# A decoder kernel: the step sizes of its state-space stage from a 32-column projection

## The reference

```
zxbcdt = X @ W_in.T
z, xBC, dt = split(zxbcdt)            # 1024 z, 1152 xBC, 16 dt
dt = softplus(dt + dt_bias)           # step sizes, one for each of 16 heads
xBC = silu(conv1d(xBC) + conv_b)      # 4 taps
x, B, C = split(xBC)
h[t] = h[t-1] * exp(dt[t] * A) + dt[t] * B[t] * x[t]
y[t] = C[t] . h[t] + D * x[t]
y = rmsnorm(y * silu(z)) * norm_w
out = y @ W_out.T
```

## Time and profile before

| | |
|---|---|
| median of three runs | 2119.28 us |
| profiled execution | 2113.45 us |
| its span on the core | 2111.7 us |
| PE busy | 1977.2 us, 94% |
| DVE busy | 1455.6 us, 69% |
| ACT busy | 1222.7 us, 58% |
| POOL busy | 390.4 us, 18% |
| instructions | 40222 |

### The profile page before, as it was taken

How to read it: one execution, slowest core, us unless ns; L and a number is a source line. 1 busy time by engine, 2 the same in 40 slices (tenths; PEclk the granted TensorE clock), 3 DMA queues, 4 the chain that set the end, 5 groups by cost and what they waited for, 6 DMA issues and landing times. The chain is left out here.

```text
span 2111.7 us, 40222 instructions
## 1 busy us (share of the span) xinstructions
PE 1977.2 (94%) x13484; PEld 1339.6 (63%) x13484; DVE 1455.6 (69%) x2887; ACT 1222.7 (58%) x3068; POOL 390.4 (18%) x596
## 2 busy tenths in 40 slices
PE   7899999999999999858999999999999999889988
PEld 6667676767676767535566666666665655478853
DVE  7978787878786868525757676757576767556438
ACT  4435354444444453316878787878778786546614
POOL 1110111111111010230122222222212132200006
PEclk9999999999999999888999999999999999999999
DMA  6122222222221313232334333333333332631157
GB/s 211 53 59 79 60 79 60 79 52 87 50 88 41 98 27 91 81 113 63 101 81 121 81 112 86 104 91 105 98 91 101 88 97 71 190 135 61 60 189 269
DMA packets 120291, 200.72 MB, mean 95 GB/s; under 512 B 23072, under 2 KB 44576, under 8 KB 120096
## 3 DMA queue, kind: packets, MB, share of 16 engines
q1 hardware_dynamic: 110880, 179.20, 28.3%
q0 software_dynamic: 9216, 18.89, 3.6%
HBM read 117.27 MB, written 29.88 MB: 70 GB/s over the span
## 5 line engine op out<-in xcount | busy, mean ns | idle before, releaser
L1751 ACT ACTIVATE a_shared<-a_shared,a_mx 128x512 f32<-128x512 f32 x512 | 341.6, 670 | 57.2 <-DVE a_mx L1812 57.2
L1744 ACT ACTIVATE a_probs<-a_scores 128x512 f32<-128x512 f32 x512 | 292.4, 605 | 96.5 <-PE a_scores L1954 94.4
L1812 DVE TENSOR_REDUCE a_mx<-a_shared 128x1 f32<-128x512 f32 x512 | 318.6, 682 | 14.4 <-PE a_shared L1938 13.4
L934 PE MATMUL m_proj<-m_xt_hi,link 128*128 128x512 f32 x576 | 241.8, 420 | 18.9 <-DVE m_xt_lo L655 11.0
L1954 PE MATMUL a_scores<-a_qs,a_ks 98*128 98x512 f32 x512 | 218.9, 435 | 21.6 <-ACT a_probs L1744 17.9
L1938 PE MATMUL a_shared<-a_ks,a_qs 96*128 96x512 f32 x512 | 216.2, 434 | 17.6 <-ACT a_shared L1751 13.4
L935 PE MATMUL m_proj<-m_xt_lo,link 128*128 128x512 f32 x576 | 230.7, 401 | 0.0
L936 PE MATMUL m_proj<-m_xt_hi,link 128*128 128x512 f32 x576 | 230.2, 400 | 0.0
L1076 PE MATMUL m_outp<-m_wout,m_g 128*128 128x512 f32 x512 | 226.3, 600 | 2.7 <-issue 2.7
L1912 PE MATMUL a_shared<-link 128*128 128x512 f32 x768 | 189.5, 399 | 18.6 <-POOL a_ks L1684 15.7
L463 ACT ACTIVATE m_acc<-m_proj,m_cb,m_cw 128x512 f32<-128x512 f32 x72 | 58.2, 818 | 254.0 <-PE m_proj L936 253.8
(11 more groups left out here) (259 smaller groups left out, 3437.1 us busy)
## 6 DMA issues: line engine op xcount, KB each, us to landing
m_dec<-step_decay SPq DMA_DIRECT2D x64, 256.0 KB, 4.0
a_qs<-link SPq DMA_DIRECT2D x256, 64.0 KB, 2.1
m_ce<-run_decay SPq DMA_DIRECT2D x128, 112.0 KB, 3.6
a_ks<-a_k_hi POOLq DMA_DIRECT2D x192, 64.0 KB, 2.4
e_x<-x SPq DMA_DIRECT2D x11, 1024.0 KB, 5.5
m_xt_in<-x_t_in SPq DMA_DIRECT2D x8, 1024.0 KB, 7.8
m_x_tok<-x_in SPq DMA_DIRECT2D x8, 1024.0 KB, 5.5
x<-m_x_tok SPq DMA_DIRECT2D x32, 256.0 KB, 2.2
```

The costliest lines, as they stand in the source:

```text
L934: pe.matmul(bank[:, :], wh, xt_hi[:, k, :], start=(k == 0), stop=False)
L1744: act.activation(probs[:, n % 2, h, :], scores[t.score_bank(n, h)][:, :], ACT.Exp, scale=-1.0).then_inc(exp_ready, 1)
L1751: act.activation(scored[:, :], scored[:, :], ACT.Exp, scale=-1.0, bias=mx[:, i % 2, j, h:h + 1], accum_out=den[:, i, j, h:h + 1]).then_inc ...
L1812: dve.tensor_reduce(mx[:, i % 2, j, h:h + 1], bank(what)[:, :], AX.X, ALU.min).then_inc(mx_ready, 1)
```

## The change

The step-size tile gets weights of its own, `w_dt`: for each slice 16 columns of high parts and beside them 16 of low parts. A slice takes two products, with high x and with low x, so eight in all (`dt_proj`). The bank then holds 32 rows, the upper 16 from high weights and the lower from low weights. ACT copies all 32. `turn_steps` multiplies by `pair_sum`, a 32 x 16 matrix with two ones in each column, instead of transposing, which turns the rows and adds the halves. DVE makes `w_dt` at the head from chunk 0, POOL makes `pair_sum` from the identity, and `SET` is 9. The product of low weights with low x is now included.

```
-        SET = 8
+        SET = 9
...
+            pool.tensor_tensor(pair_sum[:, :], ident[0:2 * NH, 0:NH], ident[0:2 * NH, NH:2 * NH], ALU.add
+                               ).then_inc(const, 1)
...
-                act.activation(dt_ch[0:NH, :], proj[0][0:NH, :], ACT.Copy).then_inc(dt_read, 1)
+                act.activation(dt_ch, proj[0][0:2 * NH, :], ACT.Copy).then_inc(dt_read, 1)
...
                 chain.link(dve.tensor_copy(win_hi[:, :, lo:hi], staging[c]))
+                if c == 0:
+                    dve.tensor_copy(w_dt[:, :, 0:NH], staging[c][:, :, 0:NH])
+                    dve.tensor_tensor(w_dt[:, :, NH:2 * NH], staging[c][:, :, 0:NH], win_hi[:, :, 0:NH], ALU.subtract)
...
+            def dt_proj(b, first):
+                if first:
+                    pe.wait_ge(w_used, 1)
+                else:
+                    pe.wait_ge(z_ready, at(b, XT_TILES, -1))
+                for k in range(KT):
+                    pe.wait_ge(xt_split, at(b, KT, k + 1))
+                    pe.matmul(proj[0][0:2 * NH, :], w_dt[:, k, :], xt_hi[:, k, :], start=(k == 0), stop=False)
+                    ins = pe.matmul(proj[0][0:2 * NH, :], w_dt[:, k, :], xt_lo[:, k, :], start=False,
+                                    stop=(k == KT - 1))
                 ins.then_inc(tile_done, 1)
...
                 for c in range(CH):
-                    ins = pe.transpose(turn[:, c * NH:(c + 1) * NH], dt_ch[0:NH, c * P:(c + 1) * P],
-                                       ident[0:NH, 0:NH])
+                    ins = pe.matmul(turn[:, c * NH:(c + 1) * NH], dt_ch[:, c * P:(c + 1) * P], pair_sum[:, :],
+                                    start=True, stop=True)
...
             def head(b):
-                in_proj(b, True, 0, 0)
+                dt_proj(b, True)
...
                     elif more:
-                        in_proj(b + 1, False, 0, 0)
+                        dt_proj(b + 1, False)
```

More of the change, by code:

```diff
@@ L138, in mamba_stage @@
                           for n in range(2))
+        w_dt = sb("w_dt", [P, KT, 2 * NH], F32R)
+        pair_sum = sb("pair_sum", [2 * NH, NH])
         wout = sb("wout", [P, XT_TILES, DM])
@@ L158, in mamba_stage @@
         x_tok = sb("x_tok", [P, TT, DM])
-        dt_ch = xt_in[0:32, 0, :]
+        dt_ch = xt_in[0:2 * NH, 0, :]
         dt = sb("dt", [P, CH, NH])
@@ L916, in in_proj @@
                 if first:
-                    pe.wait_ge(w_used, next(c for c, (lo, hi) in enumerate(CHUNKS) if col + (P if n else NH) <= hi) + 1)
+                    pe.wait_ge(w_used, next(c for c, (lo, hi) in enumerate(CHUNKS) if col + P <= hi) + 1)
                 if n < 2:
@@ L930, in in_proj @@
                 for k in range(KT):
-                    if n == 0:
-                        pe.wait_ge(xt_split, at(b, KT, k + 1))
                     wh, wl = win_hi[:, k, col:col + P], win_lo[:, k, col:col + P]
@@ L936, in in_proj @@
                     ins = pe.matmul(bank[:, :], wl, xt_hi[:, k, :], start=False, stop=(k == KT - 1))
+                ins.then_inc(tile_done, 1)
+            def dt_proj(b, first):
[8 more added lines that the diff above has]
+                                    stop=(k == KT - 1))
                 ins.then_inc(tile_done, 1)
```

## The result

The changed kernel took 2109.95 us in the median of 16 runs (2103.76 to 2116.74), the kernel before 2119.33 in as many. The ratio is 0.9964, 95% interval 0.9954 to 0.9975: 7.6 us faster, 5.3 to 9.7 (the two medians lie 9.4 apart). The forecast was 2115.0, 4.3 us faster, with a range of 2111.5 to 2121. The profiled execution hides the gain: it took 2112.64 (span 2110.9), 0.8 us less than the one before, so that a comparison of the two profiles' ends alone says almost nothing. One has to compare piece by piece.

What follows compares the result with a forecast made beforehand. PE sets the pace in the state-space stage. Savings of 0.48 (head), 0.89 (turn 1), 1.36 (turns 2 to 5) and 1.54 (turns 6 and 7) sum to 4.3 us, from 2119.28 to 2115.0; range 2111.5 to 2121.

Steps and rivals of the forecast that it cites:

- The way and the path at full clock: Settled turns 2 to 5: shorter tile, dearer turn, wait before the gate tile absorbed; 0.34 us saved each, 1.36 together.
- Tile: Step-size tile, settled turns: four of twelve products go, DVE's slices each 0.60 us limit the gain; 0.55 us saved.
- Turn: Turn of the step sizes, every turn: four transposes become four f32 products, priced from L1063; 0.46 us added.
- rival C: Step-size turn: each f32 product costs four transposes, 1.40 us in all; sum +0.5 us, 2119.8; chance 0.12.
- The wait that covers it: Before the first gate tile: PE's 0.25 us wait for DVE's convolution goes, so 0.34 us is saved a settled turn.
- Rival A: Step-size turn: cheap, 31 ns a record; 6.0 us saved in all, 2113.3; chance 0.15.
- D: Rival: DVE does not follow in the turn, only PE's own gain counts; 2.5 us saved, 2116.8; chance 0.12.
- Turn 1 and the head: First sequence: fewer tile products at 1.2 GHz save 0.48 us at the head and 0.89 in turn 1.
- Rival B: All turns: narrow products let the clock fall each time; +5.2 us, 2124.5; chance 0.13.
- Turns 6 and 7: These two turns stay at the low clock: tile 0.98 us shorter, 0.77 saved each after turn and wait, 1.54 together.

Runs made afterwards that it cites:

- e5: Changed kernel with DVE's split of the next sequence's x moved ahead of the gating of group 2; ratio to the kernel before 0.9934.
- e3: Changed kernel with the tile's four high-x products first, then the four with low x; ratio to the kernel before 0.9944.
- e1: Kernel before with only the step-size turn changed, four f32 products with 32 rows instead of four transposes; ratio 0.9999.
- e8: Changed kernel run again, unchanged; ratio to the kernel before 0.9949.
- e2: Changed kernel with the turn as four transposes of 32 rows and DVE adding the halves; ratio to the kernel before 0.9947.
- e6: Changed kernel with DVE's x split earlier, the turn by transposes and the sum on DVE; 2104.45 us, ratio to the kernel before 0.9915.
- e4: Changed kernel with 128 weight columns in the step-size tile instead of 32, still eight products; 2113.3 us, ratio to the kernel before 0.9969.
- e9: Kernel before with the four products of L1042 done twice in each sequence; ratio 1.0005.
- e12: Changed kernel with the four products of L1060 done twice in each sequence; 2120.8 us, ratio to the kernel before 1.0008.

## Why the prediction was right, and what it missed

The way and the path at full clock were right. The sum was too small, 4.3 us against 7.6, and the time landed at the lower end of the range.

**Tile.** 2.38 us against a predicted 2.40 (2.95 less 0.55), DVE's slices in the way as said; e5 shows it by taking them away. Narrow products come at 0.23 us like wide ones in a full queue (four in 0.94 in e3), and at 0.26 behind a wait.

**Turn.** Mis-sized: 0.46 was taken from L1063, 0.64 was measured. The eight records come 0.12 us apart, not 0.10. The trace before had another row that gives the price, L1042, with fewer than 128 contraction rows as here, though with 128 moving columns:

```profile
241.03 1.16 PE L1042 MATMUL m_added<-m_ct,m_bt 64*128 64x128 f32 x8
242.02 0.41 PE L1045 MATMUL m_y<-m_ident,m_bt 64*128 64x64 f32 x4
```

That is eight records in 0.99 us. The prediction's reason for its row, that the weight loads fill the time with few moving columns, was not tested. The Trainium skill's factor of four for FP32 transposes ("TensorE: Matmul & The Clock Gate", Terms) would have given 1.40 and rival C. Measured is 0.99 / 0.35, a factor of 2.8: between the row chosen and the rule.

**The wait that covers it.** Mis-sized the other way: 0.25 was read from the brackets; 0.51 was there (e1). The two errors nearly cancel, which is luck: PE behind the turn is 0.6 - 0.64, some 0.04 later, not 0.09 earlier, and takes back the wait: 0.45 a sequence at full clock, predicted 0.34. The mechanism held; rivals A, C and D did not come. Rival A's 6.0 us is nearer to the 7.6 than the forecast is, but its cheap turn is not there: the turn costs 0.64 more. D erred on DVE, which did follow the tile: counted from the tile's start its convolution (L645, now L652) begins at 7.90 us, where it was 8.47 (turn 2: 217.62 and 220.22).

**Turn 1 and the head.** From the head's turn to turn 1 the first sequence took 94.77 us before and 94.76 after, but 92.9 to 95.6 over the profiles of these two kernels, since low stretches of the clock lie in it. The head's turn came at 15.68 us where it was 17.77, because the clock rose over 2 us earlier in that execution (products come 0.23 us apart from 12.57 on, in the kernel before from 14.90 on); e8 has 17.11, and the kernel before 17.6 to 17.9 in the others. The prediction had kept the rise at 14.6. The turn at the head ends at 16.67 and 18.10 in the changed kernel's two profiles, at 17.93 to 18.24 in the four before. So the predicted 0.48 and 0.89 can't be told from this. Up to turn 1 the changed kernel's profiles are 1.9 us ahead in the mean (110.3 against 112.3), but the four before differ by 2.5 us among each other.

**The clock.** Here the prediction's picture was incomplete. Its step on turns 6 and 7 took for granted that the same two turns stay slow. Rival B, more slow turns through narrow products, had the wrong sign: there were fewer. Two things moved. A slow turn costs 1.0 us instead of 1.6, since at 1.2 GHz eight products, 0.43 us each, leave no time in which PE waits for DVE's slices, while at full clock it does; in e5, where PE waits at neither clock, a slow turn costs 1.5 again. And in the kernel before a slow turn brought the next: its four profiles have 2, 6, 2 and 3 slow turns, the changed kernel's two have 1 and 2. Over all its profiles and those of e2 to e6, 13 of 42 turns are slow, in the kernel before 13 of 24.

With these counts: 3.25 x 1.56 = 5.1 us lost before, 1.5 x 1.02 = 1.5 after, 3.5 us less. At turn 7 the changed kernel's two profiles are at 755.06 and 756.01, the four before at 761.80 to 768.57, 8.1 us ahead in the mean. Those 8.1 are 3.5 for slow turns, 6 x 0.45 = 2.7 for the sequences and the 1.9 up to turn 1. Behind turn 7 the change shortens only the way to one more gate tile. There the two profiles take 1355.8 and 1356.9 us and the four before 1349.6 to 1353.4. e2, with the changed tile too, takes 1347.9 there. That scatter is larger than the gain, so the profiles can't be added up to the measured 7.6; that this part is the same in the mean is assumed, not shown.

The granted clock of the runs gives a second estimate, without profiles. Over 172 executions of this study, each compared with the others of its kernel and session, one with a mean granted clock 0.001 lower takes 1.2 us longer. The clock is 0.9734 over the changed kernel's 16 runs, 0.9709 over 23 runs of the kernel before beside e1 to e4, which by this is 3 us of the 7.6. The same working gives 3.8 us back of the 6 added in e9, and 3.2 on top of the 6 in e12; the ratios say 5 and 3.

So the step that failed is "**Turns 6 and 7**", as a term for what the clock takes: it priced two fixed slow turns, where the change made slow turns cheaper and rarer. By both estimates two fifths to a half of the measured gain comes from there. That the repeat depends on the length is shown by e9 and e12, which move it both ways, and by the count over all profiles. Why 109.2 us is the length that repeats is not shown; e1, with 109.3 after turn 2 and then a turn at full clock, says that little is needed to leave it. Whether the width of the products has a small effect on the clock of its own, e4 leaves open.

## What to carry to other kernels

When removing products from a queue, look at the rate at which their operands are made, and read a wait from the starts of the instructions around it, since the idle time of a pipelined engine shows only what is left beyond the overlap. Where a loop's length is constant to 0.01 us, a fall of the clock at one place can repeat in every round; then a change of half a microsecond or one a round may be worth much more or less than its work (here 3.2 us of shorter sequences came with a gain of 7.6, and 6 us of added work cost 1 us in one kernel and 9 to 11 in the other), and a second length of the loop should be run before a gain is put down to the edit. Compare several profiles, round by round; the end of one profile can hide a gain of 0.4%, since a stage that nobody touched varied by 6 us.

## What the runs showed of the hardware that was not expected

An f32 product with 32 rows, 128 weight columns and 16 moving columns takes 0.25 us in PE's queue (four in 0.99), a transpose of 32 rows to 32 columns 0.09. A weight load of 32 columns is recorded with 107 ns, one of 128 with 188 (changed kernel, turn 2). A product behind a wait takes 0.26 against 0.33 us to the next start, which may come from this; in a full queue both come every 0.23. A stretch at 1.2 GHz lasted 3.4 us in a slow turn (turn 6 of the kernel before, about 642.8 to 646.2) and began next to the start of the step-size tile, behind products of 64 columns; in a program in which such a sequence lasts 109.2 us it came back in every sequence, up to six times in a row.
